# Attention and FFN on one core: layer-norm statistics by single batches, weight halves at other batches, more zero matmuls at the start

## What is computed

```python
def xattn(q, k, v, gamma):          # (16, 128, 256) each; 8 heads of 16 channels
    qh = q.reshape(B, 8, 16, L); kh = k.reshape(B, 8, 16, L); vh = v.reshape(B, 8, 16, L)
    qk = jnp.einsum('bhdq,bhdl->bhql', qh, kh) / sqrt(16)
    return gamma * jnp.einsum('bhql,bhdl->bhdq', softmax(qk), vh).reshape(B, 128, L)

def ffn(x, gate_w, up_w, down_w, gate_scale, up_scale, down_scale):   # 256 -> 768 -> 256
    gate = silu((x @ fp8(gate_w)) * gate_scale)
    up = (x @ fp8(up_w)) * up_scale
    return ((gate * up) @ fp8(down_w)) * down_scale

x = x + tanh(g_xattn) * xattn(layernorm(x), ctx, ctx, gamma)
x = x + tanh(g_ffn) * ffn(layernorm(x), ...)
```

## Time and profile before

| | us |
|---|---|
| median of three runs | 216.98 |
| the runs | 216.81, 216.98, 222.78 |
| profiled execution, its time | 217.2 |
| its span (first to last instruction) | 215.4 |
| PE busy in the span | 199.4 (93%) |
| DVE busy | 162.9 (76%) |
| POOL busy | 141.2 (66%) |
| ACT busy | 117.1 (54%) |

### The profile page before, as it was taken

The page is one execution under the profiler, slowest core; times in us unless marked ns, Lnnn a source line. Parts: engine busy times, 40 slices in busy tenths (PEclk is TensorE's granted clock), DMA queues, the critical chain, the costliest instruction groups (busy, mean ns, idle before and its releaser), DMA issues.

```text
span 215.4 us, 4656 instructions
## 1 busy us (share of the span) xinstructions
PE 199.4 (93%) x1745; PEld 124.9 (58%) x1745; DVE 162.9 (76%) x315; ACT 117.1 (54%) x210; POOL 141.2 (66%) x157
## 2 busy tenths in 40 slices
PE   6589799999999999889999997999989999999992
PEld 4247465665565566555566565445756766766581
DVE  4998989987889898845997755153965667765885
ACT  2003656675676577533777566277727654754450
POOL 3790449669699299999999500394474699657440
PEclk9955999999999999967999999999999999999999
DMA  5899921110532223330231232211230002002032
GB/s 172 226 329 362 324 30 51 49 28 28 146 112 73 87 92 96 100 99 6 58 126 42 61 120 62 97 52 50 76 106 27 2 0 97 3 2 97 0 100 97
DMA packets 23959, 19.85 MB, mean 92 GB/s; under 512 B 4096, under 2 KB 23424, under 8 KB 23936
## 3 DMA queue, kind: packets, MB, share of 16 engines
q1 hardware_dynamic: 23936, 19.54, 30.0%
HBM read 13.11 MB, written 6.42 MB: 91 GB/s over the span
## 4 chain that ended last, share of the span: by engine, by line
PE 78%; DVE 8%; POOL 4%; issue 4%; ACT 3%; DMA 1%; POOLq 0%; DVEq 0%; ACTq 0%
PE ps L731 18%; PE ps L719 18%; PE ps L775 17%; PE ps L752 13%; PE ps L835 9%; PE ps L740 3%; DVE nm L542 3%; ACT p_t L468 1%; POOL x_sb L389 1%; POOL u_n L386 1%; DMA x_sb<-in_x 1%; DVE stats L530 1%; PE ps L762 1%; POOL km L352 1%; ACT xn L497 1%
## 5 line engine op out<-in xcount | busy, mean ns | idle before, releaser
L542 DVE TENSOR_REDUCE nm<-ps 128x2 f32<-128x512 f32 x128 | 81.0, 685 | 15.0 <-PE ps L719 14.9
L468 ACT ACTIVATE p_t<-ps 128x512 f32<-128x512 f32 x128 | 68.1, 603 | 43.7 <-PE ps L731 43.6
L719 PE MATMUL ps<-km,qn 32*128 32x512 f32 x256 | 78.7, 689 | 5.7 <-POOL qn L359 3.5
L731 PE MATMUL ps<-qm,km 32*128 32x256 f32 x512 | 79.1, 413 | 2.7 <-ACT p_t L468 1.3
L731 PEld LDWEIGHTS ps<-qm,km 32*128 32x128 f32 x512 | 53.2, 193 | 15.0 <-issue 6.4
L775 PE MATMUL ps<-w_exp,w_gu 128*128 128x512 f16 x192 | 45.2, 380 | 1.3 <-DVE w_exp L583 1.3
L447 POOL TENSOR_TENSOR f_lo<-fu,f_hi 128x512 fp32r<-128x512 f32 x23 | 29.3, 1278 | 21.2 <-ACT f_hi L486 21.2
L719 PEld LDWEIGHTS ps<-km,qn 32*128 32x128 f32 x256 | 22.6, 197 | 17.8 <-issue 13.4
L752 PE MATMUL ps<-p_t,v_t 128*32 128x256 f32 x512 | 31.7, 389 | 0.4 <-ACT p_t L468 0.4
L652 DVE SCALAR_TENSOR_TENSOR ga<-th,ps 128x512 f32<-128x512 f32 x24 | 16.4, 682 | 18.7 <-ACT th L481 18.7
L775 PEld LDWEIGHTS ps<-w_exp,w_gu 128*128 128x128 f16 x192 | 17.2, 98 | 21.2 <-DVE w_exp L583 1.5
(11 more groups left out here) (60 smaller groups left out, 177.8 us busy)
## 6 DMA issues: line engine op xcount, KB each, us to landing
u_scr<-u_sb SPq DMA_DIRECT2D x32, 128.0 KB
u_n<-u_scr SPq DMA_DIRECT2D x16, 128.0 KB
r_n<-r_scr SPq DMA_DIRECT2D x16, 128.0 KB
out_x<-p_t SPq DMA_DIRECT2D x16, 128.0 KB, 1.8
x_sb<-in_x SPq DMA_DIRECT2D x3, 512.0 KB, 7.7
c_sb<-in_ctx SPq DMA_DIRECT2D x3, 512.0 KB, 7.6
ct_sb<-in_ctx_t SPq DMA_DIRECT2D x3, 512.0 KB, 6.6
w_all<-in_L_ffn_gate_w SPq DMA_DIRECT2D x1, 768.0 KB, 8.9
```

Of the source, the lines that this page charges most:

```text
L468: nc.scalar.activation(p_t[:, b % 2, i, :], ps[:, bank_of["t", n][0], :], ACT.Exp, scale=DH ** -0.5).then_inc(exp_ok, 1)
L542: nc.vector.tensor_reduce(to[:, g, :, 0], ps[:, bank_of["s", n][0], :].rearrange("p (e l) -> p e l", e=PAR), axis=AX.X, op=ALU.max, negate ...
L719: nc.tensor.matmul(ps[:, bank, :], qn[rows, b % 3, P * t:P * (t + 1)], km[rows, b % 4].rearrange("p e l -> p (e l)"), start=True, stop=Tru ...
L731: last = nc.tensor.matmul(ps[:, bank, L * e:L * (e + 1)], km[rows, b % 4, 1 - e, P * t:P * (t + 1)], qm[rows, b % 2, e, :], start=True, st ...
```

## The change

It has five parts:

- `stats_group` becomes `stats_batches(lo, hi)`, and a table STATS says which batches stand in which `between`: two each at b = 0 and 1, one each at 2 to 6 and at 8, two at 9. The first four batches stay ahead of the loop.
- HALF_BINADES is now 2, 3, 4, 5, 6, 8 (it was 1, 2, 4, 6, 8, 10) and HALF_ROUNDED 3, 4, 6, 7, 8, 10 (it was 2, 4, 6, 8, 10, 11).
- The negated mean of batch 0 is made by DVE, and no longer by POOL. `queries` waits for it by semaphores of its own, nm0_ok and nm1_ok.
- The scales of `between` stand at b = 10 and no longer at 9.
- 22 zero matmuls in place of 17.

```diff
-HALF_BINADES = (1, 2, 4, 6, 8, 10)
-HALF_ROUNDED = (2, 4, 6, 8, 10, 11)
+STATS = {0: (4, 6), 1: (6, 8), 2: (8, 9), 3: (9, 10), 4: (10, 11), 5: (11, 12), 6: (12, 13), 8: (13, 14), 9: (14, 16)}
+HALF_BINADES = (2, 3, 4, 5, 6, 8)
+HALF_ROUNDED = (3, 4, 6, 7, 8, 10)
...
-                nc.gpsimd.tensor_scalar(neg_m[:, lo:hi], mv[:, lo:hi, 0], -1.0, None, ALU.mult).then_inc(r1_ok, 1)
+                if n > 0:
+                    nc.gpsimd.tensor_scalar(neg_m[:, lo:hi], mv[:, lo:hi, 0], -1.0, None, ALU.mult).then_inc(nm1_ok, 1)
...
             def queries(b):
-                pool.wait_ge(r1_ok, 2 * group_of(b) + 2)
+                pool.wait_ge(r1_ok, group_of(b) + 1)
+                if group_of(b) > 0:
+                    pool.wait_ge(nm1_ok, group_of(b))
+                else:
+                    pool.wait_ge(nm0_ok, 1)
...
-            def stats_group(n):
-                lo, hi = GROUPS[n]
-                v.wait_ge(x_in[n], 16)
+            def stats_batches(lo, hi):
+                v.wait_ge(x_in[group_of(lo)], 16)
...
-            stats_group(0)
+            stats_batches(0, 1)
+            v.wait_ge(ag1_ok, 1)
+            nc.vector.tensor_scalar(neg_m[:, 0:1], mv[:, 0, 0:1], -1.0, None, ALU.mult).then_inc(nm0_ok, 1)
...
-            stats_group(1)
+            stats_batches(1, 4)
...
-                if b in (1, 3, 7):
-                    stats_group({1: 2, 3: 3, 7: 4}[b])
+                if b in STATS:
+                    stats_batches(*STATS[b])
...
-                if b == 9:
+                if b == 10:
...
-            for _ in range(17):
+            for _ in range(22):
```

More of the change, by code:

```diff
@@ L187, in build @@
         r1_ok = sem("r1_ok")
+        nm0_ok = sem("nm0_ok")
+        nm1_ok = sem("nm1_ok")
         qn_ok = sem("qn_ok")
```

## The result

The changed kernel is slower, by less than 2%: the ratio of its time to that of before is 1.0144, with a 95% interval of 1.0082 to 1.0207. Its four executions took 220.04, 220.11, 222.29 and 222.56 us, with a median of 221.2; the profiled one is that of 222.29, with a span of 220.5 against 215.4. The forecast was 220.0, in a range from 215.2 to 222.5.

A forecast was written before the change was run, and what follows sets the result against it. PE holds 78% of the wait chain, with POOL's queries setting many of its turns in the batch loop. 217.2 + 0.8 (POOL's chain) + 1.1 (masks) + 0.9 (clock) = 220.0 us, range 215.2 to 222.5.

The forecast's parts named there:

- turn 2: PE's pair of transposes of batch 2's maxima: expected at 25.8 instead of 26.96, 1.2 earlier through less DVE work.
- POOL's chain: Loop: roundings in neighbouring batches make POOL's steps 8.7 where PE needs 6.9; after turn 2's gain, +0.8 us at turn 13.
- the clock in the loop: PE stalls of about 1.8 ahead of turns 6, 9, 10, 11, 12 lower its clock: +0.9 us, bounds 0 and 3.2.
- turn 13: PE's transposes of batch 13's maxima: expected sign 112.6 to 114.6; before 111 the prediction is wrong as a whole.
- Masks against POOL: Loop: DVE's exponent masks of halves 1 to 5 delay a busy POOL by 0.22 each, +1.1 us; bounds nothing and 0.55 each.
- turns 9 to 12 each 8.7 or more apart and each 2.1 behind its query: Sign in the loop that POOL runs without a pause from context 7 to query 13; steps near 7 would refute it.
- DVE's gaps: DVE's extra work per batch is free up to 1.2 us; rival, chance 0.15: these gaps were the real loss, 215.3 us.
- I charge against it what the start gains: Batch 0: the 0.8 of added DVE statistics is charged against the start's gain, taken as 0.3.
- A fall at one of the first three is eaten by the spare 1.8 of each following step: Loop: clock falls ahead of turns 6, 9 or 10 cost nothing; ahead of turn 11 1.4, of turn 12 3.2.
- the rival of the last stall: Rival, chance 0.13: the clock falls ahead of turn 12 and stays low past turn 13; 222.3 us.
- The full exchange of the port: Rival, chance 0.10: each of five DVE masks costs POOL its whole 0.55, 2.75 in place of 1.1; 221.65 us.
- The early clock: Rival, chance 0.05: PE keeps 2.4 GHz through the first two batches, winning 2 us more; 213 us.

The follow-up runs named there:

- stalls filled: The changed kernel with 12 zero matmuls ahead of the first scores of batches 7, 10, 11, 12 and 13; ratio to before 1.0089.
- small masks: The changed kernel with each exponent mask over 8 of 768 columns, POOL filling the rest with ones; executions 217.04, 221.26, 221.36 and 271.1 us.
- the statistics alone: The kernel before with only the statistics distributed over single batches and the scales at batch 10; ratio 0.9999.
- the halves spread: The changed kernel with halves rounded at 2, 4, 6, 11, 14, 15, masks moved, statistics of batches 4 to 7 at batch 1; 211.4 us, ratio 0.9736.

## Why the prediction was right, and where its sizes were off

Summed by its own steps, against the profiled executions:

| step | forecast | measured |
|---|---|---|
| turn 2 | 25.8 | 26.55 |
| turn 2 to 13, POOL's chain and masks | 87.9 (86.8 and 1.1) | 87.2: stalls filled, less 0.6 for the zero matmuls |
| the clock in the loop | 0.9 | 3.0 |
| turn 13 against before's 111.77 | +2.8 | +5.0 |
| the time | 220.0 | 222.3 profiled; 220.0 to 222.6 |

The direction and the large term were right, and the median of 221.2 is 1.2 above the forecast. But turn 13 came at 116.8, outside the 112.6 to 114.6 that were to be the sign of it, and one step of the clock's term was wrong in kind. The difference lies in turn 2 (0.75) and the clock (2.1), against 0.7 on the chain the other way.

- **POOL's chain**: right in kind and size. Turns 5, 8 and 11 stand 2.1 behind queries 6, 9 and 12. The steps of POOL were 8.93, 8.92, 8.60 and 8.64 with a rounding, forecast 8.7 and a mask's share, and 8.90 with attention, forecast 8.8. Two roundings in a row are no novelty of the change: those of batches 10 and 11 followed each other before as well, with attention at 9 ahead of them. Now it is batches 3 and 4, and then 6 to 8, with attention and the rounding of 10 right behind. The sign "turns 9 to 12 each 8.7 or more apart and each 2.1 behind its query" failed: they are 8.56, 7.44 and 9.04 apart, since a fall of the clock puts turns 9 and 10 1.5 behind POOL.
- **Masks against POOL**: forecast 0.22 each, five times, 1.1. Measured in the changed kernel 0.2 (the first rounding step, 2.97 for 2.77), three times 0.31 (keys 1.40 for 1.09) and 0.14 (the copy of context 7, 0.55 for 0.41): 1.27. The run with small masks, where all of them are back at their lengths alone, shows that it is the masks. The 0.14 is no cost of the change, since the copies beside the masks of before took 0.55 and 0.56 as well; without it, it is 1.13. One mask of before also met a busy POOL: the power at 88.87 took 1.32 beside it, and 1.04 elsewhere. The bound of the full 0.55 was not reached.
- **DVE's gaps**: the rule that under 1.2 us of extra work is free held from batch 1 on: the step from turn 1 to 2 fell from 8.36 to 7.19, by the 1.2 of the forecast. It did not hold at batch 0. Turn 2 came only 0.3 earlier and not 1.2, because the 0.8 at batch 0 delayed turn 1. This is the first mis-sized step, "I charge against it what the start gains". The start gained 0.1 (first scores at 5.70 and not 5.83, since the zero matmuls ended at 5.77) where 0.3 was taken, and the statistics cost turn 1 0.9. The working argued that PE, at the lower clock, fills the stretch itself; but turn 1 waits for DVE's maxima, and these stood behind the statistics.
- **The clock**: that stalls of PE would bring it down in the loop was right. They were three of 1.2 to 1.5 and not five of 1.8. What failed is the step "A fall at one of the first three is eaten by the spare 1.8 of each following step". The fall ahead of turn 6 was not eaten. The step behind it has no rounding, so POOL has no backlog there: it stands 3.47 for PE ahead of the copy of context 7, and turn 6, 0.45 late, and turn 7, 8.0 behind it where 6.9 is undisturbed, made that copy and all that follows 1.6 late. The run with a stall of 1.52 and no fall there shows the same 1.6. The fall ahead of turn 9 was nearly eaten: POOL waited 0.24 for PE ahead of the copy of context 10. The fall ahead of turn 12, priced at 3.2, cost 1.2: 0.4 at turn 12 and 0.8 in the next step (8.05, where it is 7.25 with the stalls filled). That is 3.0 in all.
- **Luck**: the profiled 222.3 is the number of the rival of the last stall, but only 1.2 of it come from that fall. And the mean of 0.9 over five places stood for a quantity that differs from one execution to the next; that two executions hit 220.0 and 220.1 is no proof of it, as no profile shows where the clock fell in them.
- **The rivals**: POOL did cost more in a row than apart, so DVE's gaps were not the real loss (the statistics alone gave 0.9999). The full exchange of the port did not occur. The early clock, 2 us by my estimate, is worth at most 1.2 by the scatter of the run with the halves spread.

## To carry to other kernels

An engine off the critical path that feeds it once per round has a budget per round: add its works up round by round, from the wait that starts them to the result that is waited for, and put no two long ones in neighbouring rounds, nor ahead of another long one. Spreading the small works of the engine next to it brought nothing that the time could tell (0.9999), and half a microsecond in the profile once the down weights were out of the way. A delay of the other engine is absorbed only in rounds where the feeding engine has a backlog; in a round where it waits, the delay is passed on whole. Work that has a later deadline than the wait in the code says (here the down weights) should be moved by the deadline of its first reader, and the wait with it.

## What was not expected of the hardware

- A DVE instruction over 8 columns, 0.15 us by itself, took 1.12 behind a running POOL instruction, and 1.50 where it had 768 columns; POOL lost 0.31 behind it.
- Stalls of PE of 1.52, 1.51 and 1.23 us were each followed by a stretch at 1.2 GHz, and with zero matmuls of 1.49 us in their place there was none. But a stall of 1.52 in the run with the statistics at batch 1 again, and one of 1.22 in the run with small masks, at the same place, were followed by none. At the start 20 such matmuls in a wait of 2.2 us only put the fall off.
- Executions of the same kernel differ in the mean granted clock: the changed kernel took 220.0 to 222.6 us with one from 0.977 to 0.937.
